# A fused graph-network kernel: a loop of 28 passes written out in full

## The chip, the cores and the metric

The kernel runs on one core of a Trainium2 chip. The metric is the device time of one execution in microseconds (us). Before the change the median of three runs was 2906.12 us (2905.11 to 2912.86). Each of the core's engines has its own instruction stream: TensorE (PE) does the matrix products and the transposes, VectorE (DVE), ScalarE (ACT) and GpSimd (POOL) the elementwise work, SyncE (SP) issues the transfers. The engines meet only through semaphores.

## The reference

128 graphs of 128 nodes with 384 features (`x`), and an adjacency matrix for each (`adj`). Two blocks follow one another, each with a residual and a layer norm:

```python
x = layernorm(x + gnn0(x, adj))   # two layers:
    # u    = h (h W_left^T)^T / sqrt(384) above and on the diagonal, h (h W_right^T)^T below
    # att  = exp(u) * adj, rows divided by their sum
    # h    = relu(layer_norm(att @ (h W_lin^T + b)) * a + b')
x = layernorm(x + gnn1(x, adj))   # attention, 12 heads of 32:
    # p    = softmax(q k^T / sqrt(384) + 2 adj);  out = (p v) Wo^T + bo
```

## The kernel before

**Tiles.** Four graphs make a group, so there are 32 groups. An engine's program is a sequence of *passes*. Pass `it` works on block 0 (called l0 in the code) of group `it`, on block 1 (l1) of group `it - 1`, and finishes the last part (the tail) of block 1 of group `it - 2`. So 34 passes (0 to 33) do 32 groups, and the first and the last passes are incomplete. Products are made of float16 pairs (hi and lo, three matmuls for one product) accumulated in PSUM; ACT reads a product into the hi part, DVE computes the lo part.

**Order.** Within a pass the order of every engine's operations is written out by hand in that engine's function `body(p)`. PE begins a pass with `nl(p, 0, 0)`, nine matmuls of 128x512 (line 1251), then `pv(p, 3)`, the last attention product of the tail, and a little later `to(p, 3)`, three transposes of `o` (line 1261). It ends the pass with `ctx(p, 1, 0)` to `ctx(p, 1, 3)`, matmuls of 128x386. DVE begins a pass with `rs_of(p, 3)`, a reciprocal (line 874) and a small product (line 877) for the softmax sums, and makes `o` of it in `pv` (line 889). In the middle of the pass `rs_of(p, 1)` and `pv(p, 1)` do the same for PE's `to(p, 1)`. POOL's program holds, among others, `folds(p, 2)` (line 464) and right after it `xt(p, 1)` (line 380), which subtracts 128x512 elements into `hT_lo` for the group to come.

**The loop.** The function `passes` calls `body` for passes 0, 1 and 2, then opens a loop with four passes as its body (7 iterations: passes 3 to 30), then calls `body` for 31, 32 and 33. Each of the five engines runs this loop by itself: each has the branch and the loop register of its own, and there is no barrier between them. A wait in a pass is on a semaphore's running count, `group * per_group + n`. In the loop the group is an expression in the loop's register; in the passes outside it is a number. Also the addresses of the transfers contain it. Where a wait value must be in a register of its own, `await_apart` puts it there:

```python
def await_apart(self, eng, sig, n):
    value = sig.upto(self.group(sig), n)
    if not isinstance(value, int):
        value = eng.snap(eng.to_reg(value), min_val=1)
    eng.wait_ge(sig.sem, 1)
    eng.wait_ge(sig.sem, value)
```

Of the kernel before, what the change touches and what calls it, by code (L numbers as in the profile page):

```python
# [6 lines left out]
GROUPS = GRAPHS // GROUP  # L7
# [23 lines left out]
def program(nc, x, xT, adj, adjT, weights, biases, ln_cols, ln_rows, out):  # L31
# [5 lines left out]
    with ExitStack() as stack:  # L37
# [208 lines left out]
        def passes(eng, body, head=None):  # L246

            if head:
                head()
            first = Pass(0, 0, l1=False, tail=False, before=prologue, setup=True)  # L250
            body(first)
            second = Pass(1, 1, tail=False, before=first)
            body(second)
            body(Pass(2, 0, before=second))
            with eng.Fori(3, GROUPS - 4, 4) as it:
                for n in range(4):
                    body(Pass(it + n, (n + 1) % 2, before=Pass(it + n - 1, n % 2)))
            body(Pass(GROUPS - 1, 1, nxt=False, before=Pass(GROUPS - 2, 0)))
            body(Pass(GROUPS, 0, l0=False, nxt=False, before=Pass(GROUPS - 1, 1, nxt=False)))
            body(Pass(GROUPS + 1, 1, l0=False, l1=False, nxt=False,  # L260
                      before=Pass(GROUPS, 0, l0=False, nxt=False)))
# [11 lines left out]
        def _(sp):  # L273
# [25 lines left out]
            def body(p):  # L299
# [24 lines left out]
                for b in range(3):  # L324
                    store(p, b)

            passes(sp, body)
            for i in range(2):
                sp.wait_ge(out_st[i].sem, out_st[i].upto(GROUPS - 1, 32))
# [3 lines left out]
        def _(pool):  # L333
# [191 lines left out]
            def head():  # L525
# [3 lines left out]
                mask_right(prologue)  # L529

            passes(pool, body, head)


        @block.scalar
        def _(act):
# [245 lines left out]
            def head():  # L781
                weight(0)
                weight(1)
                for k in range(KB):
                    xt(prologue, k)

            passes(act, body, head)


# [759 lines left out]
```

## Time and profile before

| | |
|---|---|
| median of three runs | 2906.12 us |
| the profiled execution, its time | 2910.63 us |
| its span in the profile | 2908.9 us |
| PE busy | 2811.0 us, 97% |
| DVE, ACT, POOL busy | 84%, 61%, 57% |
| mean granted clock of TensorE | 0.987 of full speed |
| data moved | 113.03 MB, 39 GB/s |

The span is the stretch that the profiler's records cover; it is 1.7 us shorter than the time of that same execution. The profile calls time "issue" in which an engine waited for nothing that it shows. Register, branch and semaphore instructions are in none of the busy times.

### The profile page before, as it was taken

Reading aid. Unit: us, or ns where it says so; the run is one execution under the profiler, and the core shown is the slowest. Engines: PE = TensorE matmul, PEld = TensorE weight load, DVE = VectorE, ACT = ScalarE, POOL = GpSimd, SP = SyncE. Lnnn points to the kernel's source line nnn. Section 1 sums busy time; section 2 is a strip of 40 time slices with the busy share of each in tenths; the row PEclk is TensorE's granted clock in tenths of the full one; section 3 lists DMA queues with packets and bytes.
Section 4 is the critical chain, followed back from the end, with each engine's and each line's share of the span. In section 5 each row is a group of like instructions: output and inputs, shape, how many; then the busy total and the mean of one; then the engine's idle time right before and its main releaser. Section 6 shows DMA issues by size and latency. Waiting matters only on the chain.

```text
span 2908.9 us, 74992 instructions
## 1 busy us (share of the span) xinstructions
PE 2811.0 (97%) x24768; PEld 1794.6 (62%) x24768; DVE 2433.9 (84%) x8042; ACT 1773.5 (61%) x4107; POOL 1662.0 (57%) x2097
## 2 busy tenths in 40 slices
PE   7999999999999999999999999999999999999996
PEld 4566666666666566665666656666566656666654
DVE  4888988888888789887888878897888888888886
ACT  4565666556676556665566655566565666655664
POOL 2555566556565556664565645656555655556564
PEclk9999999999999999999999999999999999999997
DMA  4001011101011010111110110101101011101000
GB/s 149 30 31 45 21 45 42 42 32 45 21 42 42 32 45 21 45 42 38 36 42 24 43 43 31 45 21 46 39 34 43 31 35 42 42 31 45 21 27 21
DMA packets 56061, 113.03 MB, mean 39 GB/s; under 512 B 4944, under 2 KB 37712, under 8 KB 55632
## 3 DMA queue, kind: packets, MB, share of 16 engines
q1 hardware_dynamic: 55632, 107.76, 11.0%
q8 instruction: 214, 3.51, 0.5%
q14 instruction: 215, 1.76, 0.2%
HBM read 82.58 MB, written 25.17 MB: 37 GB/s over the span
## 4 chain that ended last, share of the span: by engine, by line
PE 80%; DVE 10%; issue 6%; ACT 3%; DVEq 0%; POOL 0%; DMA 0%; SPq 0%; POOLq 0%; ACTq 0%
PE psum L1251 58%; PE psum L1261 9%; PE psum L1312 9%; PE psum L1405 3%; DVE z L1017 2%; PE psum L1379 1%; ACT w L597 1%; DVE nT_lo L814 1%; DVE rs L877 1%; DVE pT_lo L812 1%; DVE hT_lo L1038 1%; DVE o L889 1%; ACT qk_hi L537 1%; ACT pT_hi L537 1%; DVE st L916 1%
## 5 line engine op out<-in xcount | busy, mean ns | idle before, releaser
L597 ACT ACTIVATE w<-s,nmax 128x128 f32<-128x128 f32 x1536 | 479.4, 401 | 1.9 <-DVE nmax L847 1.9
L1251 PE MATMUL psum<-hT_hi,w_hi 128*128 128x512 f16 x1152 | 442.8, 384 | 35.4 <-issue 19.7
L1251 PE MATMUL psum<-hT_hi,w_lo 128*128 128x512 f16 x1152 | 442.3, 384 | 0.0
L1251 PE MATMUL psum<-hT_lo,w_hi 128*128 128x512 f16 x1152 | 442.2, 384 | 0.0
L537 ACT ACTIVATE nT_hi<-psum 128x512 f16<-128x512 f32 x384 | 230.1, 599 | 306.1 <-PE psum L1251 306.1
L847 DVE CUSTOM_DVE_ANT_0 s<-psum,adj 128x128 f32<-128x128 f32 x1536 | 350.6, 285 | 33.3 <-PE psum L1379 30.6
L464 POOL TENSOR_TENSOR fold<-fold 128x384 f32<-128x384 f32 (+4 forms) x640 | 344.0, 538 | 50.2
L464 POOL TENSOR_TENSOR fold<-s 128x768 f32<-128x768 f32 x128 | 244.2, 1908 | 194.7 <-DVE nmax L847 194.7
L388 POOL TENSOR_TENSOR hl_lo<-hl_raw,hl_hi 128x384 fp32r<-128x384 f32 x256 | 246.6, 968 | 144.9 <-ACT hl_hi L537 140.7
L812 DVE TENSOR_TENSOR pT_lo<-psum,pT_hi 128x512 f16<-128x512 f32 x384 | 251.5, 683 | 35.1 <-ACT pT_hi L537 34.7
L537 ACT ACTIVATE pT_hi<-psum 128x512 f16<-128x512 f32 x384 | 221.7, 596 | 84.3 <-PE psum L1261 84.3
L814 DVE SCALAR_TENSOR_TENSOR nT_lo<-psum,nT_hi 128x512 f16<-128x512 f32 x384 | 256.3, 681 | 12.4 <-ACT nT_hi L537 12.3
L431 POOL TENSOR_TENSOR yrstd<-yvar,pw 128x4 f32<-128x4 f32 x32 | 32.4, 1013 | 397.8 <-DVE yvar L997 397.8
L537 ACT ACTIVATE z<-psum,rden 128x384 f32<-128x384 f32 x256 | 138.3, 579 | 197.4 <-DVE rden L963 197.4
L1251 PE MATMUL psum<-w_hi,hT_lo 128*128 128x384 f16 x768 | 250.3, 326 | 0.0
L1251 PE MATMUL psum<-w_lo,hT_hi 128*128 128x384 f16 x768 | 250.3, 326 | 0.0
L1251 PE MATMUL psum<-w_hi,hT_hi 128*128 128x384 f16 x768 | 250.3, 326 | 0.0
L1251 PE MATMUL psum<-xT_hi,w_hi 128*128 128x512 f16 x576 | 219.8, 382 | 0.0
L1251 PE MATMUL psum<-xT_lo,w_hi 128*128 128x512 f16 x576 | 219.1, 380 | 0.0
L1251 PE MATMUL psum<-xT_hi,w_lo 128*128 128x512 f16 x576 | 218.8, 380 | 0.0
L1251 PEld LDWEIGHTS psum<-hT_hi,w_hi 128*128 128x128 f16 x1152 | 113.2, 98 | 165.1 <-issue 43.0
L1261 PE MATMUL psum<-ident,w 128*128 128x128 f32 x1536 | 208.7, 276 | 2.6 <-DVE nmax L847 2.0
(133 smaller groups left out, 8066.6 us busy)
## 6 DMA issues: line engine op xcount, KB each, us to landing
xTin<-xT SPq DMA_DIRECT2D x32, 768.0 KB, 4.5
xres<-x SPq DMA_DIRECT2D x32, 768.0 KB, 4.6
out<-y SPq DMA_DIRECT2D x128, 192.0 KB, 1.9
adjn<-adj SPq DMA_DIRECT2D x32, 256.0 KB, 4.8
adjT_sb<-adjT SPq DMA_DIRECT2D x32, 256.0 KB, 5.0
adj<-adj SPq DMA_DIRECT2D x32, 256.0 KB, 2.7
x<-weights SPq DMA_DIRECT2D x4, 576.0 KB, 5.3
s<-weights SPq DMA_DIRECT2D x3, 576.0 KB, 6.3
```

Of the source, the lines that this page charges most:

```text
L388: nc.gpsimd.tensor_tensor(hl_lo[:, b, 0:FEAT], hl_raw[:, b], hl_hi[:, b, 0:FEAT].bitcast(f32), ALU.subtract).then_inc(hlr_lo[l].sem, 1)
L464: nc.gpsimd.tensor_tensor(fold[:, :, 0:n], src[:, :, 0:n], src[:, :, n:2 * n], ALU.add)\
L537: return nc.scalar.activation(dst, src, ACT.Copy, scale=scale)
L597: last = nc.scalar.activation(w[:, m], s[b % 2][:, m], ACT.Exp, bias=nmax[b % 2][:, m:m + 1], scale=-1.0)
L812: nc.vector.tensor_tensor(dst, src, rounded, ALU.subtract).then_inc(done.sem, 1)
L814: nc.vector.scalar_tensor_tensor(dst, src, scale, rounded, ALU.mult, ALU.subtract)\
L847: last = nc.vector.tensor_tensor_reduce(out=s[b % 2][:, m], in0=psum[:, SC[j], c * TOK:(c + 1) * TOK], in1=adj2[:, b], scale=-1.0 / TEMPER ...
L1017: nc.vector.tensor_scalar(z[:, b], z[:, b], rstd[0][:, b:b + 1], nmr[:, b:b + 1], ALU.mult, ALU.add)\
L1251: last = mm(dst, a, b, start=(i == 0), stop=(i == total - 1))
L1261: last = transpose(dst[:, n * 128:(n + 1) * 128], src, ident[:])
L1312: last = mm(dst, a, m, start=(i == 0), stop=(i == len(terms) - 1))
L1405: last = mm(dst[:, n * VCOL:(n + 1) * VCOL], a, m, start=(i == 0), stop=(i == 2))
```

## The change

The loop of seven iterations of four passes becomes 28 passes one after another in the program of each engine. The pass number is a number everywhere, so the wait values and the addresses of the transfers are constants; in `await_apart` the branch for a register is never taken. The parity of a pass (which of two buffers it uses) is the same as before. No operation, buffer, or order within a pass is changed.

```diff
-            with eng.Fori(3, GROUPS - 4, 4) as it:
-                for n in range(4):
-                    body(Pass(it + n, (n + 1) % 2, before=Pass(it + n - 1, n % 2)))
+            for it in range(3, GROUPS - 1):
+                body(Pass(it, it % 2, before=Pass(it - 1, 1 - it % 2)))
```

## Rows read from the trace of the kernel before

**Rows 1.** The page: busy times, and the chain that ended last by engine.

```profile
PE 2811.0 (97%) x24768; PEld 1794.6 (62%) x24768; DVE 2433.9 (84%) x8042; ACT 1773.5 (61%) x4107; POOL 1662.0 (57%) x2097
...
PE 80%; DVE 10%; issue 6%; ACT 3%; DVEq 0%; POOL 0%; DMA 0%; SPq 0%; POOLq 0%; ACTq 0%
```

**Rows 2.** List of waits, whole span: us in total, times, longest us.

```profile
PE psum L1251 <- issue: 20.0, 7, 4.4
```

**Rows 3.** Windows from pass start to pass start: passes 2, 3, 5 to 7, 30.

```profile
core 0: us, PE busy (x) PEld busy (x) DVE busy (x) ACT busy (x) POOL busy (x), PEclk, DMA share, GB/s
162.04:248.96 86.92, 86.67 (x775) 55.78 (x775) 74.31 (x251) 54.86 (x129) 51.86 (x66) 1.00 0.11 38
248.96:337.24 88.28, 87.18 (x775) 55.63 (x775) 76.16 (x251) 54.66 (x128) 51.92 (x66) 1.00 0.11 37
...
424.97:512.68 87.71, 86.85 (x776) 55.79 (x775) 75.73 (x252) 54.87 (x128) 51.89 (x66) 1.00 0.11 37
512.68:602.85 90.17, 86.84 (x775) 55.92 (x775) 77.73 (x261) 56.98 (x132) 54.60 (x69) 1.00 0.11 37
602.85:693.00 90.15, 87.35 (x774) 55.76 (x775) 73.72 (x244) 53.18 (x124) 49.19 (x63) 1.00 0.12 37
...
2653.14:2740.65 87.51, 86.68 (x776) 55.92 (x775) 75.31 (x252) 54.87 (x128) 51.93 (x66) 1.00 0.11 38
```

**Rows 4.** Windows by iteration of four passes: the seventh, and the sum of all.

```profile
2387.01:2740.65 353.64, 349.99 (x3097) 223.85 (x3097) 300.37 (x996) 217.47 (x508) 204.67 (x258) 0.99 0.11 37
sum 2491.69, PE 2443.45 PEld 1564.62 DVE 2121.45 ACT 1538.38 POOL 1453.51; mean PE 349.06 PEld 223.52 DVE 303.06 ACT 219.77 POOL 207.64
```

**Rows 5.** Timeline of PE at the first and second jump: start, duration, operation, [idle before].

```profile
600.00 0.34 PE L1251 MATMUL psum<-hl_hi,e_lo 128*128 128x386 f32 x1
602.85 0.39 PE L1251 MATMUL psum<-hT_hi,w_hi 128*128 128x512 f16 x1 [2.51 <-issue]
...
959.96 0.63 PE L1251 MATMUL psum<-hT_hi,w_hi 128*128 128x512 f16 x1
```

**Rows 6.** Window behind the jump that follows the fourth iteration.

```profile
1674.33:1679.10 4.77, 4.77 (x42) 2.29 (x43) 0.00 (x0) 0.60 (x1) 0.00 (x0) 0.50 0.13 45
```

**Rows 7.** Timeline of DVE behind the first jump; PE's waits in pass 7, then 5.

```profile
607.83 0.23 DVE L874 RECIPROCAL rs<-psum 128x12 f32<-128x12 f32 x1 [4.49 <-issue]
...
610.98 0.55 DVE L889 TENSOR_TENSOR o<-psum,rs 128x384 f32<-128x384 f32 x1
...
PE psum L1261 <- DVE o L889: 1.8, 2, 1.3
...
PE psum L1261 <- DVE o L889: 0.5, 1, 0.5
```

**Rows 8.** Timelines of POOL and DVE: passes 5, 2, 1; line 877 in pass 7.

```profile
493.16 1.16 POOL L380 TENSOR_TENSOR hT_lo<-xTin,hT_hi 128x512 f16<-128x512 f32 x1
493.30 1.04 DVE L877 SCALAR_TENSOR_TENSOR rs<-live,rs 128x12 f32<-128x12 f32 x1
...
230.27 0.17 DVE L877 SCALAR_TENSOR_TENSOR rs<-live,rs 128x12 f32<-128x12 f32 x1
230.32 1.16 POOL L380 TENSOR_TENSOR hT_lo<-xTin,hT_hi 128x512 f16<-128x512 f32 x1
...
142.65 1.13 DVE L877 SCALAR_TENSOR_TENSOR rs<-live,rs 128x12 f32<-128x12 f32 x1
...
L877 DVE SCALAR_TENSOR_TENSOR rs<-live,rs x4: 170/171/1041, 608.1 to 683.5; 128x12 f32<-128x12 f32 x4
```

**Rows 9.** Instruction queues: packets, MB, share; whole span, then pass 2.

```profile
q8 instruction: 214, 3.51, 0.5%
q14 instruction: 215, 1.76, 0.2%
...
q8 instruction: 6, 0.10, 0.4%
q14 instruction: 4, 0.03, 0.2%
```

## The prediction

> **What bounds the kernel now.** I read the page first: TensorE (PE) is busy 97% of the span and carries 80% of the chain that ended last, VectorE (DVE) 10%, and 6% is "issue", time in which an engine waited for nothing that the profile shows [rows 1]. So a microsecond is only won where PE stands still. The list of waits says where it does: PE waited at line 1251 for "issue" 7 times, 20.0 us in all, 4.4 us at the longest [rows 2]. Seven is a number that the loop has too: 7 iterations of four passes, so 6 jumps back.
>
> To see whether these are the jumps I cut the trace at the starts of the passes. A pass starts with the first matmul of nl(p, 0, 0), right after the last hl product of the pass before; in the timeline that is 602.85 for pass 7 [rows 5]. The windows from start to start are the heart of this prediction [rows 3]. Pass 5, inside an iteration, takes 87.71 us. Pass 6, whose end is the first jump back, takes 90.17, and pass 7, the first after the jump, 90.15. PE's busy time is 86.8 to 87.4 in all of them: the work is the same, and what differs is that it stands still. Pass 2, the full pass that is already straight code before the loop, takes 86.92, and pass 3, the loop's first, 88.28. Pass 30, the last of the loop, after which nothing jumps, takes 87.51.
>
> The same by iterations [rows 4]: the 28 passes of the loop take 2491.69 us together, 88.99 each; the last four, without a jump at their end, 353.64. Against 28 passes of 87.71 (2455.88) that is 35.8 us too many. This is the pot that the change can take from.
>
> **The change, part by part.** *The jumps.* At the first one the last ctx matmul starts at 600.00 and the next matmul at 602.85, with 2.51 us of idle time put down to "issue" [rows 5]: PE had no operand to wait for. A stall of that kind is not all. DVE jumps as well: its next instruction, the reciprocal of line 874, starts 4.49 us after it fell idle, at 607.83, and its output o comes at 610.98 [rows 7]. The transposes to(p, 3) at the head of pass 7 need it, so PE waits again: 1.8 us for o in two waits of pass 7, the longest 1.3, where pass 5 has one wait for o, of 0.5 [rows 7]. So a jump costs 90.17 - 87.71 = 2.46 before the pass and 90.15 - 87.71 = 2.44 in it, 4.9 us together [rows 3].
>
> Later jumps cost more, for a second reason. A matmul of 128x512 takes 0.39 us behind the first jump and 0.63 behind the second, at 959.96 [rows 5]; in the 4.77 us after the jump at 1674.33 the granted clock is 0.50, the lower level, 1.2 GHz [rows 6], after a PE that had stood still. Behind the first jump the window of pass 7 shows 1.00 [rows 3]. I need not split these prices: the sum over the 28 passes holds them all. Six jumps and the entry into the loop make 35.8 us, 6.0 for a jump if they carry everything. All of it goes: straight code has no jump, PE doesn't stand still there, and with no idle time there the clock has no reason of this kind to fall.
>
> The Trainium skill, Advanced Engine Details and Errata, section Control Flow Timing, gives about 108 ns for a compare-and-branch. By that figure six jumps would be worth some 0.65 us and the change nothing that can be told. The Trainium skill's page Runtime: NRT & Kernel Launch, section Instruction fetch mechanics, says instead that a taken branch whose target is not in the window of blocks held must wait for a fetch. The rows side with the second: the gap is 2.51 us and more [rows 5].
>
> *The register work.* Inside the loop each wait value is computed in registers, in straight code it is a constant. These instructions don't count as busy, and I can only bound what they cost by comparing passes: the loop's pass 5 against the straight pass 2, 87.71 - 86.92 = 0.79 us at most, and 28 of these are 22.1 us [rows 3]. Where do the 0.79 come from? Almost all of it is one event. In pass 5 POOL starts the subtraction hT_lo (line 380) at 493.16, it runs 1.16 us, and the tiny DVE operation rs of line 877, 12 columns, starts at 493.30 and takes 1.04 us: it ends when POOL's does. In pass 2 the DVE operation starts at 230.27, before POOL's at 230.32, and takes 0.17 [rows 8]. The output o, and with it PE's transposes to(p, 1), come about 1.04 - 0.17 = 0.87 us later in pass 5, and PE's one wait of 0.5 us for o is there [rows 7]. This is an order of two starts, not register work on the path. The straight pass 1 shows that constants don't settle it: there rs starts at 142.65 and takes 1.13 [rows 8], the same collision. In pass 7 the longest of the four is again 1.041. So of the two straight passes that have this POOL operation one escapes, by 0.05 us; in the loop's the DVE operation comes 0.14 us too late. I take one straight pass in five as escaping and the rest as pass 5: 0.2 x 86.92 + 0.8 x 87.71 = 87.55 us. Otherwise register work is hidden, PE's under its queue of matmuls, the others' under PE's. Without that cover it would show in pass 5 as idle PE, of which it has 87.71 - 86.85 = 0.86 us, all causes together [rows 3]; so 0.86 us a pass is the most that it can be worth in any case.
>
> *What is added.* Straight code must fetch all its instructions once. So does the loop: over the whole run there are 214 + 215 = 429 instruction packets, in the straight pass 2 there are 6 + 4 = 10 [rows 9]. A body fetched once would be 10 passes of code or so, some 100 packets; 429 are 12.6 for each of the 34 passes. So the body is fetched again in each iteration, and the fetch lies beside the work of passes 2 and 5, whose PE doesn't stand still. I cost it at nothing; if this cover were gone, the nearest row for a fetch on the path is the gap of 2.5 us. A smaller price has its nearest row in pass 3, 88.28, the longest pass without a jump at either end. DMAs, buffers, order of the engines' programs stay as they are; no queue is passed by anything.
>
> **The sum.** 28 x 87.55 = 2451.4 us, against 2491.7: a gain of 40.3 us. The profiled execution took 2910.63 us with a span of 2908.9; after the change I expect a span of 2868.6. The median of the runs is 2906.12, 4.5 below the profiled one. Taking the same gain off the median gives 2865.8 us.
> Bounds: with every pass like pass 2, 28 x 86.92 = 2433.8, gain 57.9, 2848.2 us. With every pass like pass 5, gain 35.8, 2870.3. With every pass like pass 3, 28 x 88.28 = 2471.8, gain 19.9, 2886.3.
>
> **Rivals.** *Every pass becomes like pass 2* (2848 us, down from about 2857): the collision of POOL and DVE is gone because the order of the two starts turns over everywhere. For it: pass 2 is straight code and complete. Against it: pass 1, straight too, collides, and the margins are 0.05 us one way and the other.
> *Straight code has small stalls of its own* (2877 to 2895, at pass 3's price 2886): blocks of instructions arrive a little late, at DVE above all, which starts its pass closest to need. For it: pass 3 is 0.57 us longer than pass 5 and has no jump before it. Against it: pass 2 is not.
> *Slower*: PE's fetch of a new block is exposed in each pass. One such stall of 2.5 us a pass is 28 x 2.5 = 70 us, less the 35.8 gained: 2940 us. It decides from 35.8 / 28 = 1.28 us a pass on. For it: an unrolled program never runs an instruction twice. Against it: neither does the loop, to judge by its packets [rows 9], and passes 2 and 5 show no such stall.
> *The jump is not the cause*: the branch itself is cheap and the stall belongs to something that stays, say a wait of every fourth pass on a buffer that the profile doesn't name. Then the passes of 90.17 and 90.15 us stay as they are, the sum over the 28 stays 2491.7, and the time 2906 us. For it: only that "issue" names no culprit. Against it: passes 3 to 6 run the same code, and only the one with the jump stops. The Trainium skill's figure in Control Flow Timing is on this rival's side.
>
> **How the numbers follow.** The forecast (2857 to 2877) gets 0.68, every pass like pass 2 0.14, small stalls 0.12, the jump not being the cause 0.03, slower 0.03. The predicted time is 2866 us. The range is to leave out no more than 2 in 10: from 2847, which takes in the rival below, to 2877, which leaves out the small stalls and beyond. A measurement of this kernel tells about 0.3% (9 us) from no change. Faster by over 0.3%: 0.94; within 0.3%: 0.03; slower by over 0.3%: 0.03.
>
> **What would show it.** In the profile after: no wait for "issue" of over 1 us at line 1251 between 100 and 2740 us; all passes from start to start between 86.9 and 87.8 us, with none of 90; PE's share at 98% and the granted clock at 1.00 from 100 us to the last passes; instruction packets per pass as in pass 2. A line 877 that takes about 1.0 us once in most passes confirms the collision, about 0.17 everywhere the first rival. The prediction is wrong if straight passes differ among each other by a microsecond, or if "issue" appears at PE in other places: then it is the fetch.

## The result

The straight program takes 2869.89 us (median of four runs, 2866.59 to 2871.08). The kernel before, with one more run made beside it, has a median of 2907.42 us over its four runs. The ratio is 0.9866, with a 95% interval of 0.9851 to 0.9882: faster by 1.3%. Predicted were 2866 us, range 2847 to 2877. The profiled execution has a span of 2868.0 us, where 2868.6 was expected.

The page of the kernel after, to be held against [rows 1]:

```profile
span 2868.0 us, 69803 instructions
...
PE 2794.6 (97%) x24768; PEld 1790.0 (62%) x24768; DVE 2406.5 (84%) x8042; ACT 1770.5 (62%) x4107; POOL 1657.6 (58%) x2097
...
q8 instruction: 199, 3.26, 0.5%
q14 instruction: 145, 1.19, 0.1%
...
PE 86%; DVE 10%; ACT 2%; issue 1%; POOL 0%; DMA 0%; DVEq 0%; SPq 0%; POOLq 0%; ACTq 0%
```

"Issue" fell from 6% to 1% of the chain, and the instruction packets from 429 to 344: the program executes fewer instructions, and it has no jump that would need a fetch. Line numbers are one lower than before. PE's waits of the kernel after, whole span (us in total, times, longest):

```profile
PE psum L1260 <- DVE o L888: 23.3, 32, 4.1
...
PE psum L1250 <- issue: 0.3, 1, 0.3
```

The line that said 20.0 us in 7 waits [rows 2] says 0.3 in one. So the seventh wait of before was a small one that is no jump; the six at the jumps were 2.51 to 4.39 us. The windows of passes 2, 4, 5, 7, 21 and 30, from start to start, answer to [rows 3]:

```profile
161.57:248.49 86.92, 86.67 (x775) 55.76 (x775) 74.22 (x251) 54.86 (x129) 51.79 (x66) 1.00 0.11 38
336.13:423.67 87.54, 86.75 (x776) 55.76 (x775) 74.75 (x251) 54.84 (x130) 51.73 (x66) 1.00 0.11 38
423.67:511.25 87.58, 86.74 (x775) 55.75 (x775) 74.83 (x251) 54.84 (x129) 51.78 (x66) 1.00 0.11 37
598.78:686.37 87.59, 86.75 (x775) 55.74 (x775) 74.88 (x251) 54.84 (x129) 51.78 (x66) 1.00 0.11 37
1825.18:1912.11 86.93, 86.68 (x775) 55.75 (x775) 74.14 (x251) 54.85 (x130) 51.81 (x66) 1.00 0.12 38
2613.00:2700.58 87.58, 86.74 (x776) 55.78 (x775) 74.77 (x251) 54.86 (x130) 51.77 (x66) 1.00 0.11 38
```

Pass 7, 90.15 us behind the first jump, now takes 87.59. Of the 28 passes that were the loop, 27 take 87.52 to 87.82 us and one, pass 21, takes 86.93. All 28 together, and the stretch from 54 us, in pass 0, to 2791 us, in pass 31:

```profile
248.49:2700.58 2452.09, 2429.11 (x21674) 1561.13 (x21673) 2094.45 (x7028) 1536.01 (x3586) 1449.48 (x1821) 1.00 0.11 38
...
54.40:2791.00 2736.60, 2709.37 (x24109) 1740.27 (x24107) 2330.24 (x7804) 1710.83 (x3985) 1610.80 (x2022) 1.00 0.11 37
```

2491.69 - 2452.09 = 39.6 us of the 40.9 that the span lost lie in these passes [rows 4]. And the clock stays at its upper level, 2.4 GHz, from 54 us to 2791 us, where before it fell to 1.2 GHz behind each jump but the first [rows 6].

The collision of POOL and DVE that the prediction described is still there in pass 5:

```profile
491.74 1.15 POOL L379 TENSOR_TENSOR hT_lo<-xTin,hT_hi 128x512 f16<-128x512 f32 x1
491.88 1.04 DVE L876 SCALAR_TENSOR_TENSOR rs<-live,rs 128x12 f32<-128x12 f32 x1
```

Again DVE's tiny operation comes 0.14 us too late and ends with POOL's [rows 8]. In pass 21 it isn't hit (line 876 in that window, ns at the least, median, most):

```profile
L876 DVE SCALAR_TENSOR_TENSOR rs<-live,rs x4: 170/172/230, 1828.6 to 1902.6; 128x12 f32<-128x12 f32 x4
```

### The profile page after: what moved, and what is told of

Read it like the earlier page. It is cut to its first block, busy times and chain, and to the rows that moved or that the text cites. A ratio compares the mean times of both kernels' runs of the same rounds, so it can differ in the third digit from the quotient of the medians.

```text
span 2868.0 us, 69803 instructions
## 1 busy us (share of the span) xinstructions
PE 2794.6 (97%) x24768; PEld 1790.0 (62%) x24768; DVE 2406.5 (84%) x8042; ACT 1770.5 (62%) x4107; POOL 1657.6 (58%) x2097
## 4 chain that ended last, share of the span: by engine, by line
PE 86%; DVE 10%; ACT 2%; issue 1%; POOL 0%; DMA 0%; DVEq 0%; SPq 0%; POOLq 0%; ACTq 0%
PE psum L1250 62%; PE psum L1260 11%; PE psum L1311 9%; PE psum L1404 3%; PE psum L1378 2%; DVE z L1016 2%; DVE nT_lo L813 2%; DVE pT_lo L811 1%; DVE rs L876 1%; DVE qk_lo L813 1%; ACT qk_hi L536 1%; ACT pT_hi L536 1%; DVE st L915 1%; DVE o L888 1%; DVE y L907 1%
## 5 line engine op out<-in xcount | busy, mean ns | idle before, releaser
L846 DVE CUSTOM_DVE_ANT_0 s<-psum,adj 128x128 f32<-128x128 f32 x1536 | 341.0, 284 | 30.8 <-PE psum L1378 30.0
L1311 PE MATMUL psum<-nT_hi,hT_lo 128*128 128x256 f16 x768 | 209.3, 273 | 0.0
```

The lines of the kernel that those rows point to most:

```text
L846: last = nc.vector.tensor_tensor_reduce(out=s[b % 2][:, m], in0=psum[:, SC[j], c * TOK:(c + 1) * TOK], in1=adj2[:, b], scale=-1.0 / TEMPER ...
L1311: last = mm(dst, a, m, start=(i == 0), stop=(i == len(terms) - 1))
```

## The experiments

Nine kernels were run, all of them computing the whole reference. Spans are of the profiled execution; beside them stand the ratio of the time to that of the kernel before and its 95% interval. Comments in the diffs are added here.

### How many jumps: one and thirteen

The loop was kept and cut otherwise.

```diff
-            with eng.Fori(3, GROUPS - 4, 4) as it:
-                for n in range(4):
+            with eng.Fori(3, GROUPS - 14, 14) as it:     # two iterations of 14 passes
+                for n in range(14):
```

> The loop has two iterations of 14 passes: one jump back in place of six, and register wait values in all 28 passes as before. Theory A (the jumps made the gain, some 5.9 us each, and 0.13 us a pass is register work): span 2868.0 + 5.9 + 28 x 0.13 = 2877.5 us. Theory B (the 0.13 us a pass come from elsewhere): 2874. Theory C (register work in each pass made the gain, 1.4 us a pass): 2907, as before. In the windows A expects passes without a jump of 87.71 us, B of 87.58.

Measured: span 2878.3 us, median 2877.55, ratio 0.9886 (0.9869 to 0.9902). Windows of the pass that ends in the one jump, of the pass behind it, and of the next:

```profile
1389.06:1479.66 90.60, 87.05 (x775) 55.72 (x775) 78.28 (x261) 57.11 (x133) 54.71 (x69) 1.00 0.11 37
1479.66:1570.61 90.95, 87.36 (x774) 55.76 (x775) 73.53 (x243) 53.06 (x124) 49.00 (x63) 1.00 0.11 37
1570.61:1658.32 87.71, 86.86 (x775) 55.78 (x775) 75.82 (x252) 54.89 (x128) 51.88 (x66) 1.00 0.11 38
```

The jump costs 2.89 + 3.24 = 6.1 us over two passes of 87.71. All 28 passes compute their wait values in registers here, and the time is near the straight kernel's: theory C falls. Most undisturbed passes take 87.7 us (the extremes are 87.33 and 87.87), not 87.58, as A had it.

The same two lines, with a shorter body:

```diff
+            with eng.Fori(3, GROUPS - 2, 2) as it:       # 14 iterations of two passes
+                for n in range(2):
```

> The loop has 14 iterations of two passes: 13 jumps in place of six, the same register work. Theory A (a jump costs about 5.9 us): 2908.9 + 7 x 5.9 = span 2950 us. Theory C (register work made the gain): 2909, no change. If a shorter body of two passes is still held by an engine, so that its jump needs no fetch, a jump is cheaper: under 2920.

Measured: span 2946.0 us, ratio 1.0126 (1.0109 to 1.0143), slower than before. PE's waits in it:

```profile
PE psum L1251 <- issue: 35.4, 14, 3.0
PE psum L1261 <- DVE o L889: 35.1, 45, 4.1
```

13 jumps, 13 stalls of PE at the jump (one of the 14 waits is small and not at a jump), and DVE's o late behind them. Spans with 0, 1, 6 and 13 jumps are 2868.0, 2878.3, 2908.9 and 2946.0 us: 6.1 us a jump from one to six, 5.3 from six to thirteen. A body half as long doesn't make the jump cheaper by much. Each of the 13 jumps has its instruction fetch (below, in "What a jump waits for"), so the body of two passes is not held either.

### Which engine's jump

Each engine has its own loop, so each can be straight by itself (the diff is against the kernel before, indentation left out).

```diff
+            if eng is nc.tensor:
+                for it in range(3, GROUPS - 1):          # as in the kernel after
+                    body(Pass(it, it % 2, before=Pass(it - 1, 1 - it % 2)))
+            else:
                 with eng.Fori(3, GROUPS - 4, 4) as it:
```

> TensorE's program is straight, the other four engines loop as before. Theory A1 (the stalls of PE and DVE at a jump overlap; DVE's stall of 4.5 us alone makes PE wait at the head of the pass): PE no longer stands 2.5 us at the jump, comes to its transposes of o earlier and waits there about 2.4 + 2.5 us; span 2868.0 + 6 x 4.6 + 3.5 = 2899 us. Theory A2 (the two parts of a jump's price add, and DVE's is 2.4 us): 2868.0 + 6 x 2.4 + 3.5 = 2886.

Measured: span 2915.8 us, median 2918.34, ratio 1.0029 (1.0019 to 1.0040). With PE's jumps gone the kernel is no faster, rather a little slower. PE's waits over the whole span, then DVE's first operation behind its jump, then PE's wait in the stretch from 600 to 615 us, and a window just behind it:

```profile
PE psum L1265 <- DVE o L893: 51.1, 39, 5.0
...
607.97 0.23 DVE L878 RECIPROCAL rs<-psum 128x12 f32<-128x12 f32 x1 [5.06 <-issue]
...
PE psum L1265 <- DVE o L893: 5.0, 1, 5.0
...
611.20:614.60 3.40, 2.89 (x9) 1.45 (x10) 3.37 (x9) 0.49 (x1) 0.00 (x0) 0.50 0.00 0
```

DVE stands still 5.06 us, PE then waits 5.0 us for o in one piece, and behind that one long wait the granted clock is at 0.50. Theory A2 (the parts add) is refuted. A1 has the waits right and the time wrong: PE's six waits at the jumps are 28.4 us together, where it had 27.6, but the six passes behind the jumps are 44.4 us longer than their neighbours. The other 16 us are the clock, which A1 left out: it is at 0.50 for 37.6 us in all, from the end of these waits on, at half speed a loss of up to 18.8. Pass 7 takes 94.53 us: 6.8 more than 87.70, which is the wait of 5.0 and 3.4 us at half speed (1.7 lost).

The reverse, only PE looping (`if eng is not nc.tensor` above):

> Only TensorE loops, the other four engines are straight. PE stands still 2.5 to 4.4 us at each jump, 19.5 us in all, and o is there in time behind it. Theory A1 (the lower clock behind the jumps, which was hidden under PE's wait for o, comes to the surface: five stretches of 3.4 or 6.8 us at half speed, 13.6 us lost): span 2868.0 + 19.5 + 13.6 = 2901 us. Theory A2 (the parts add, and the clock costs nothing): 2868.0 + 19.5 = 2888.

Measured: span 2895.3 us, ratio 0.9945 (0.9928 to 0.9961). PE's wait for "issue", and the windows of passes 5, 6 and 7:

```profile
PE psum L1255 <- issue: 18.0, 7, 4.2
...
423.84:511.42 87.58, 86.75 (x776) 55.76 (x775) 74.83 (x251) 54.86 (x130) 51.82 (x66) 1.00 0.11 37
511.42:601.93 90.51, 86.90 (x776) 55.75 (x775) 77.52 (x260) 56.69 (x133) 54.68 (x69) 1.00 0.11 37
601.93:689.95 88.02, 86.92 (x775) 55.85 (x775) 72.14 (x243) 53.17 (x126) 48.79 (x63) 1.00 0.11 37
```

The 27.3 us over the straight kernel are more than the 18 us of standing still and less than A1's 33. In pass 7 only 0.44 us are left of the 2.44 [rows 3]: the other 2.0 were DVE's. The rest, 27.3 - 18.0 = 9 us, goes with the lower clock. Where it stayed up behind the jump (passes 7 and 23) the pass is 0.44 us longer than its neighbours; where it fell (11, 15, 19 and 27), 1.5 to 2.4 us. It is low for 17.1 us there in all, at half speed a loss of up to 8.5. The window behind the fourth jump of this kernel shows it:

```profile
1666.80:1672.20 5.40, 5.40 (x47) 2.58 (x48) 0.37 (x3) 0.60 (x1) 0.00 (x0) 0.50 0.11 35
```

Only DVE looping:

> Only VectorE loops, the other four engines are straight. Theory D (DVE's own stall of 5 us at the jump is all that PE feels when PE is straight): the same as with all four looping, span 2912 to 2916 us. Theory E (the stalls of ACT, POOL and SP add their share): clearly less, 2890 to 2905.

Measured: span 2918.0 us, ratio 1.0039 (1.0024 to 1.0053). DVE's own wait for "issue", PE's wait for o, and the windows of passes 6, 7 and 8:

```profile
DVE rs L878 <- issue: 27.5, 6, 4.8
...
PE psum L1265 <- DVE o L893: 52.4, 39, 4.9
...
511.28:598.85 87.57, 86.68 (x776) 55.90 (x775) 75.42 (x253) 54.88 (x128) 51.81 (x66) 1.00 0.11 38
598.85:694.48 95.63, 90.03 (x775) 56.61 (x775) 76.33 (x253) 55.15 (x128) 51.74 (x66) 0.96 0.10 35
694.48:782.26 87.78, 86.86 (x776) 55.77 (x775) 76.05 (x253) 54.91 (x128) 51.90 (x66) 1.00 0.11 37
```

One engine's loop, and the kernel is slower than with five. Theory D holds and is 2 us too low: DVE's six stalls and what follows from them explain all, no other engine's is needed. Pass 7 takes 7.9 us more than pass 8. Over the six such passes it is 45.8 us: 27.8 of PE's waits at the jumps, and 18 that go with a clock of 0.50 for 6.8 us from the end of each of them on. The other 4 us of the 50 are 0.2 us in each of the other passes.

ACT, POOL and SP looping, PE and DVE straight:

> ACT, POOL and SP loop, PE and DVE are straight. Theory D: their stalls are hidden under PE, span 2868 to 2872 us. Theory E: 2885 to 2905.

Measured: span 2867.7 us, ratio 0.9877 (0.9857 to 0.9897). Pass 7:

```profile
596.87:685.08 88.21, 86.97 (x776) 55.65 (x775) 75.08 (x252) 54.98 (x128) 51.76 (x66) 1.00 0.11 38
```

Their jumps cost 0.7 us there, and most passes without one take 87.47 to 87.53 us in this kernel, so the sum is that of the straight one. Theory D again. (One of its four executions took 8060.76 us; what held it is not known, and the ratio leaves it out.)

### The collision of POOL and DVE

In the straight kernel POOL's subtraction was moved by one place in its program, later in one run and earlier in the other:

```diff
                 folds(p, 2)
-                xt(p, 1)
                 hl(p, 1, 0)
+                xt(p, 1)
```

> Straight kernel, with POOL's subtraction xt(p, 1) moved behind hl(p, 1, 0), so that it no longer starts beside DVE's rs(1). Theory F (the collision costs PE 0.65 us in each pass that has it, 27 of 28): passes of 86.93 us, span 2868.0 - 17.5 = 2850.5. Theory G (PE's wait is passed on: xt now delays the folds of graph 3, or PE waits at the next place): 2862 to 2870.

Measured: span 2849.7 us, ratio 0.9809 (0.9793 to 0.9826). Line 876 takes 242 ns at the most in it.

```diff
+                xt(p, 1)
                 folds(p, 2)
-                xt(p, 1)
                 hl(p, 1, 0)
```

> Straight kernel, with xt(p, 1) moved ahead of folds(p, 2), into POOL's idle time of 1.9 us there. Theory F: as with the move the other way, span 2850.5 us, since folds start only some 0.3 us later. Theory G: it collides with DVE's operations on scores there, or the later folds meet rs(1) themselves: 2862 to 2870.

Measured: span 2849.2 us, median 2851.48, ratio 0.9809 (0.9792 to 0.9825). POOL in pass 5, line 876 over the whole run, and the windows of passes 5 and 30:

```profile
482.88 1.16 POOL L379 TENSOR_TENSOR hT_lo<-xTin,hT_hi 128x512 f16<-128x512 f32 x1 [1.01 <-ACT hT_hi L536]
483.99 1.82 POOL L463 TENSOR_TENSOR fold<-s 128x768 f32<-128x768 f32 x1
...
L876 DVE SCALAR_TENSOR_TENSOR rs<-live,rs x128: 170/172/248, 130.4 to 2837.2; 128x12 f32<-128x12 f32 x128
...
420.67:507.58 86.91, 86.66 (x776) 55.77 (x775) 74.06 (x251) 54.87 (x130) 51.81 (x66) 1.00 0.12 38
2594.04:2680.96 86.92, 86.67 (x775) 55.77 (x775) 74.09 (x251) 54.86 (x129) 51.84 (x66) 1.00 0.12 38
```

Of its 128 times line 876 takes 248 ns at the longest, where in the straight kernel before this move 28 of 128 took 0.87 to 1.14 us. Both places give the same, so it is the meeting with rs that cost the time, not where POOL's work stands: 18.8 us for one moved line. With both changes the kernel takes 1.9% less than before and is the fastest of the study. A pass has 86.91 - 86.66 = 0.25 us of idle PE left.

The same move in the kernel before, loop kept:

> The loop of before with xt(p, 1) moved ahead of folds(p, 2). Theory H (collision and jumps are independent): 28 passes lose their 0.6 to 0.8 us, span 2908.9 - 18.5 = 2890.4 us, passes without a jump 87.1 and less. Theory I (the collision is only one of several places where the loop's DVE is late, so that PE waits at the next one): 2898 to 2906.

Measured: span 2888.8 us, median 2890.8, ratio 0.9937 (0.9920 to 0.9953). The window of pass 5:

```profile
423.23:510.32 87.09, 86.78 (x775) 55.75 (x775) 75.11 (x252) 54.88 (x128) 51.90 (x66) 1.00 0.12 38
```

Theory H: 20.1 us, against 18.8 in the straight kernel; the two gains add up, within the spread of the executions. And with the collision gone from both, a pass of the loop without a jump takes 87.09 to 87.11 us and a straight one 86.91 to 86.92: 0.18 to 0.20 us a pass is what is left for the register work. Held against each other matmul by matmul, pass 5 of the two kernels differs at one place only. 50.8 us into the pass PE comes to the matmuls that read DVE's `hT_lo` of line 1038, in the loop has to wait, and is 0.18 us late from there on.

### What a jump waits for

The profile calls PE's stall at a jump "issue" and names no cause. Its list of DMA packets does. The packets of the two instruction queues are 199 on q8 wherever PE is straight, and 205 where PE loops with one jump, 213 to 216 with six, and 232 with 13, so q8 carries PE's instructions. Here is q8 in PE's stall at the first jump of the kernel before, and at the third (windows 600.20 to 602.85 and 1311.80 to 1316.57 us; packets, MB, share):

```profile
q8 instruction: 1, 0.02, 2.2%
...
q8 instruction: 2, 0.03, 4.9%
```

The first stall lasts from 600.34 to 602.85 us, and the packet, of 16 KB, from 600.24 to 601.16. The five kernels in which PE loops have 32 jumps, and it is the same at all of them. A packet starts at the beginning of the stall (0.5 us before to 0.3 after it), and PE goes on 1.6 to 2.5 us after it has landed. At 28 jumps it is one packet, and the stall is 2.3 to 3.0 us. At the other four two packets lie over one another and take up to 2.5 us, and these four stalls are 4.0 to 4.4 us. In DVE's stalls of the kernel where it alone loops, two packets of 8 KB on the other queue, q14, follow one another each time. In straight code the same packets pass beside the work.

## Why the prediction was right, and where it wasn't

**The pot.** 35.8 us for six jumps and the entry, all of it to be gained: right. The passes that had jumps take what their neighbours take, and the time grows with the number of jumps. Nothing came in their place: of "issue" two waits of PE are left, 0.3 and 0.7 us, and instruction fetch in straight code lies beside the work, as assumed from pass 2 and the packets.

**What a jump is made of.** Only the sum was right. The prediction split the first jump into 2.46 us before the pass (PE's stall) and 2.44 in it (DVE's lateness), as if each were its engine's price. They overlap, since PE's own pause of 2.5 to 4.4 us lies inside the time that DVE would have been late anyhow. PE's jumps alone cost 27.3 us and DVE's alone 50.0, the two and all others together 40.9. That DVE's alone cost more than all five (span 2918.0 against 2908.9) is the clock: with PE straight its whole wait comes in one piece of 4.5 to 5.0 us, and behind it the clock is low for 6.8 us in 11 of the 12 cases (3.4 in one), with no wait left to hide it. Cutting PE's loop only, the engine with 97%, would have been worth nothing. The profile before had the numbers for it: DVE idle 4.49 us, PE 2.51 [rows 5, 7].

**The clock.** With no jump on PE or DVE it doesn't fall between 54 and 2791 us. But the step "later jumps cost more, for a second reason", the lower clock, failed. Pass 15 lies behind the third jump. Here is its window, and PE's wait for o in it, to be held against pass 7 behind the first jump [rows 3, 7]:

```profile
1316.57:1406.79 90.22, 89.14 (x775) 56.19 (x775) 73.26 (x242) 52.40 (x123) 48.72 (x62) 0.97 0.12 37
...
PE psum L1261 <- DVE o L889: 0.5, 1, 0.5
```

PE works 1.8 us longer in pass 15 than in pass 7, at a mean clock of 0.97, and the pass is 0.07 us longer. The wait of 1.3 us for o at the head of pass 7 isn't there: a slower PE comes to its transposes when o is ready. The six passes behind a jump take 90.14 to 90.70 us, so the clock costs this kernel at most some 0.6 us a jump. What makes later jumps dear is PE's stall itself, 2.51 us at the first and 4.29 and 4.39 at the third and fourth, whose passes (14 and 18) take 91.96 and 92.10 us. The sum of 35.8 us was untouched by this, as it was taken from all passes.

**Register work.** "Otherwise hidden" was wrong in a small way: it is 0.13 us a pass in the change itself (87.71 to 87.58), 0.18 to 0.20 with the collision out of the way. It is DVE's: the passes without a jump take 87.78 us with only DVE looping, 87.58 with only PE looping, and 87.47 with ACT, POOL and SP looping. (The last is less than the straight kernel's since the collision takes 0.94 us there and not 1.04.) Over 27 passes 0.13 is 3.5 us. The loop's passes hold a second collision, not named so far: line 865, DVE's `live`, 128x12 too, takes 1.00 us once in each, where the median is 0.16. It costs nothing here: with ACT, POOL and SP looping it takes 1.17 us, in the very passes of 87.47.

**The collision.** The step "one straight pass in five escapes" failed too: one in 28 did, pass 21. That the mean of 87.55 us came out nearly right (2452.09 / 28 = 87.57), and the span within 0.6 us, is luck: two errors cancel, since the passes that collide are 0.13 us shorter than the pass 5 that stood for them. Counted out: with one escape and the rest at 87.71 the sum would be 2455.1, 3.7 above the forecast, and 27 passes that are 0.13 shorter take 3.5 off again. The mechanism itself, and the worth of some 0.65 us a pass, were confirmed by moving POOL's operation. The Trainium skill, SBUF — State Buffer, section SBUF: two separate sides, has the rule behind it: a DVE operation with two SBUF inputs and a POOL operation that reads SBUF exclude each other for the whole length of the one that starts first. The traces agree, 1.04 us where POOL was first by 0.14, 0.17 where DVE was.

**The rivals.** Every pass like pass 2 (2848 us) didn't happen by the change, but is where the kernel stands once one POOL line is moved (span 2849.2). Small stalls, a fetch in each pass, and a jump that isn't the cause show in no window. The Trainium skill's figure of about 108 ns for a compare-and-branch (Advanced Engine Details and Errata, Control Flow Timing) can't be what a jump costs here: 5.3 to 6.1 us were measured. The Trainium skill's warning in Runtime: NRT & Kernel Launch, Instruction fetch mechanics, that a taken branch out of the window of blocks must wait for a fetch, agrees with these runs. A packet of PE's instructions lies in each of its 32 stalls, and the stalls with two such packets are the long ones. What fills the 1.6 to 2.5 us between its landing and PE's next matmul no run shows.

## What to carry to other kernels

Cut the trace into equal units of work and compare their lengths: a unit that is longer with the same busy time has a stall, and the differences price it before anything is changed. When several engines pause at one place, the price is not the sum of what each costs alone (27.3 and 50.0 us here, 40.9 together), so removing the pause of the busiest engine alone may give nothing. And look at tiny operations with a long maximum: here a 12-column product of 0.17 us that took 1.04 beside a POOL operation was worth half as much as the whole loop.

## What was not expected of the hardware

- A loop on VectorE alone costs 50 us (span 2918.0 against 2868.0), 9 more than loops on all five engines. Six stalls of DVE of 4.6 us become waits of PE of up to 4.9 us in one piece, and behind each of them the granted clock goes to 0.50 for 6.8 us. Several short waits of PE, as in the pass of 88.21 us, left the clock at 1.00.
- The body of two passes pays nearly the full price at each jump, 5.3 us.
- PE's stall at a jump goes with its instruction packets: 2.3 to 3.0 us with one of 16 KB, 4.0 to 4.4 with two that overlap.
- A tensor operation of POOL and a 12-column one of DVE that start within 0.15 us of each other in the wrong order make DVE's last until POOL's ends, 1.04 us for 0.17, and in the straight kernel that repeats in 27 of the 28 passes, at 0.87 to 1.04 us: the order of the two starts is set by the program's timing, not drawn anew in each pass.
